# A recommendation tower on one NeuronCore: each VectorE product of 2,048 columns is written as four of 512

## The chip, the core and the metric

The kernel runs on one NeuronCore of a Trainium2 chip. TensorE multiplies matrices into PSUM, VectorE and ScalarE work element by element, GpSimd here only issues gathers from tables, and SyncE only issues DMAs. The five engines run their own instruction streams and meet through semaphores. The metric is the device time of one execution in microseconds (us); lower is better.

## What is computed

For each of 2,048 samples, 39 table rows of 32 floats are looked up. Two interaction layers form all products of the 39 fields per embedding column `d`, weight and sum them; their sums over `d` go through a three-layer perceptron. Everything is float32.

```python
e = stack([tbl_f[ids[:, f]] for f in range(39)], axis=1)          # (2048, 39, 32)
conv1 = einsum('bid,bjd,ijk->bkd', e, e, W1)                       # 39*39 pairs -> 128
hidden1, final1 = conv1[:, :64], conv1[:, 64:]
conv2 = einsum('bid,bjd,ijk->bkd', e, hidden1, W2)                 # 39*64 pairs -> 128
z = sum(concatenate([final1, conv2], axis=1), axis=2)              # (2048, 192)
h = relu(concatenate([z, dense_ctx], axis=1) @ W_top1 + b_top1)
y = relu(h @ W_top2 + b_top2) @ W_top3
```

## The kernel before

The samples are cut into 16 tiles of 128, and two tiles are a pair. A pair is worked on in four chunks (`k` = 0 to 3) of half a tile each, so there are 32 chunks. The first and the last pair are written out, and the pairs between run in hardware loops on each engine.

For `hidden1`, a chunk's values lie transposed in `x_rows[k % 2]`: 117 partitions (three copies of the 39 fields) by 2,048 columns (64 samples by 32). Three more arrays, `x_moved`, hold the same values with the fields rotated; they lie in a ring of four buffers (`CRING`). A chunk has seven steps. In steps 0 to 5 VectorE multiplies two of these four arrays (`PRODUCTS`, L658) and writes all products into one of four `blocks` buffers (`ZRING`); step 6 (L640) finishes a smaller array `last`. After each step the semaphore `multiplied` rises by one, and TensorE (`hidden_step`, L370) waits for it before its matmuls of that step; each of those four reads 512 of the 2,048 columns. VectorE runs three steps ahead of TensorE (`AHEAD`).

Between the steps VectorE also transposes the finished `hidden` of the chunk before (`turn_hidden`, L668, behind step 3), transposes a tile's embeddings (`turn_x`, L632) and copies small results. TensorE's second layer (`gram_group`, L390) waits for `hid_turned`, the signal of L668; ScalarE copies its results into `arena` (L556), from which TensorE forms the final sums (`final_sums`, L407).

All larger DMAs are issued in one fixed order by SyncE's queue, SPq. For every chunk it loads `x_rows` from a scratch array `turning` in HBM (L270), copies it within SBUF to the second and third copy (L277), waits until they have landed (L280), and issues nine DMAs of 312 KB for the three rotated `x_moved` (L290) and one for `last` (L299). For every tile it also spills the gathered embeddings to `turning` in two parts (L263) and waits for each. Its waits on computed data are these: in L286 for `multiplied` before an `x_moved` buffer is written again (for the second of the three: step 2 of the chunk before must be done; for the third: step 4), in `spill_and_turn` for `multiplied` and `last_squared` before `x_rows` is written again, and at L299 for `hid_steps`, the signal of TensorE's last step.

GpSimd issues 39 gathers per tile (L337); it starts a tile when its ids are there, VectorE has transposed the tile that lay in the buffer (`xt_ready`) and its spill has landed.

Of the kernel before, what the change touches and what calls it, by code (L numbers as in the profile page):

```python
# [33 lines left out]
ALU = mybir.AluOpType  # L34
# [4 lines left out]
D = 32  # L39
Q = 4  # L40
# [8 lines left out]
HALF = PLACES // 2  # L49
COLS = HALF * Q * D  # L50
THIRDS = 3
ROWS = THIRDS * F
# [19 lines left out]
ZRING = 4  # L72
# [15 lines left out]
def build(nc, dense, ids, tables, W_top1, b_top1, W_top2, b_top2, W_top3, W1, W2,  # L88
          fold_c, identf_c, turning, y_out):
    with ExitStack() as ctx:  # L90
        def sb(name, shape, dt):
            return ctx.enter_context(nc.sbuf_tensor(name, shape, dt))

        def sem(name):
            return ctx.enter_context(nc.semaphore(name))
# [7 lines left out]
        blocks = sb("blocks", [P, ZRING, COLS], F32)  # L103
# [71 lines left out]
        multiplied = sem("multiplied")  # L175
# [28 lines left out]
        def triples(k, p):  # L204

            if k % 2:
                return turns(k, p)
            return turns(k, p) + 2 * 16 * (1 if k == 0 and isinstance(p, int) and p == 0 else 2)
# [417 lines left out]
        def _(dve):  # L626
# [8 lines left out]
            def multiply(k, t, chunk, p):  # L635

                if t == STEPS - 1:
                    dve.wait_ge(last_moved, 16 * (chunk + 1))
                    rows = slice(LAST_AT, LAST_AT + F)
                    nc.vector.tensor_tensor(last[rows, :], x_rows[k % 2][rows, :], last[rows, :],  # L640
                                            ALU.mult).then_inc(multiplied, 1)
                    return
                if t < 3:

                    n = 3 * k + t
                    dve.wait_ge(moved[n % CRING], 16 * THIRDS * (3 * p + n // CRING + 1))
                if t == 0:
                    dve.wait_ge(tripled[k % 2], triples(k, p))
                if not (isinstance(chunk, int) and 6 * chunk + t < ZRING):

                    back = STEPS * chunk + t - ZRING + 1 if t >= ZRING else STEPS * (chunk - 1) + t + 6 - ZRING + 1
                    dve.wait_ge(hid_steps, back)

                def copy(u):
                    return x_moved[(3 * k + u - 1) % CRING][0:ROWS, :] if u else x_rows[k % 2][:, :]

                u, v = PRODUCTS[t]
                nc.vector.tensor_tensor(blocks[0:ROWS, (6 * k + t) % ZRING, :], copy(u), copy(v),  # L658
                                        ALU.mult).then_inc(multiplied, 1)

            def turn_hidden(k, chunk):

# [22 lines left out]
            def pair_body(p, first, last_pair):  # L685
                for k in range(4):
                    chunk = 4 * p + k
                    for t in range(STEPS):
                        kk, tt = (k, t + AHEAD) if t + AHEAD < STEPS else (k + 1, t + AHEAD - STEPS)
                        if not (last_pair and kk == 4):  # L690
                            multiply(kk, tt, 4 * p + kk, p)
                        if t == 0 and (k or not first):
                            turn_hidden((k - 1) % 4, chunk - 1)
                        if t == 3 and k % 2 == 0:
                            turn_x(2 * p + k // 2, k // 2, p + 1)
                        if t == 1 and k % 2 == 0 and not first:
                            final_copy(2 * p - 2 + k // 2)
                        if t == 3 and k % 2 and not first:
                            y_copy(2 * p - 2 + k // 2)
# [23 lines left out]
            for t in range(TILES):  # L723
                op = nc.vector.tensor_copy(
                    dense_rows[FIN1:FIN1 + DENSE, t * P:(t + 1) * P].rearrange("p (h r q) -> p q r h", h=2, q=Q),
                    hidden[0:DENSE, t // 8, t // 4 % 2, (t % 4) * P:(t % 4 + 1) * P].rearrange("p (q r h) -> p q r h", q=Q, h=2))
# [9 lines left out]
            for t in range(AHEAD):  # L736
                multiply(0, t, 0, 0)
# [55 lines left out]
```

## Time and profile before

| | us |
|---|---|
| median of 3 runs | 1284.77 |
| lowest and highest run | 1278.77, 1286.57 |
| span of the profiled execution | 1282.7 |
| TensorE matmul busy in it | 897.3 |
| GpSimd busy | 828.4 |
| ScalarE busy | 626.2 |
| VectorE busy | 621.8 |

The busy times are sums over the whole span; none of the four fills it. The page of the profile also follows the chain of work that ended last back from the end, step by step to what released each instruction, and gives shares of the span by engine and line.

### The profile page before, as it was taken

The page shows a single profiled execution, that of the slowest core. Times are in us where ns is not written, and L with a number is a line of the kernel's source. Part 1 is how long each engine was busy: PE and PEld are TensorE (multiplying, and loading weights), DVE is VectorE, ACT ScalarE, POOL GpSimd, SP SyncE. Part 2 cuts the span into 40 slices and gives each one's busy share as a digit, 9 for nine tenths or more (in the row PEclk, how much of TensorE's full clock was granted, in tenths as well). Part 3 has the DMA queues.
Part 4 walks back from the last instruction along what each step waited for, and adds up shares of the span by engine and source line. Part 5 has one row for each costly group of instructions (what it writes and reads, how often), then busy time and mean ns, then how long its engine had stood idle before and what let it go on. Part 6 is the DMA issues. An engine that isn't in the chain of part 4 may idle for free.

```text
span 1282.7 us, 14200 instructions
## 1 busy us (share of the span) xinstructions
PE 897.3 (70%) x4685; PEld 477.9 (37%) x4685; DVE 621.8 (48%) x401; ACT 626.2 (49%) x1553; POOL 828.4 (65%) x628
## 2 busy tenths in 40 slices
PE   3055578786767778786677787676777877687786
PEld 3011224342333435342433434343353534343366
DVE  3245254646536364555535464654536455463440
ACT  0003555553546564454646545355655444464653
POOL 7785888668884888658883888848884688810000
PEclk9557678887888888786878979688888878788888
DMA  7466756555565655555665555556555565665500
GB/s 199 63 140 139 138 136 132 128 130 126 135 140 130 133 131 128 124 133 127 144 127 128 129 131 131 128 131 138 128 133 126 126 133 122 135 143 119 120 1 1
DMA packets 145611, 159.96 MB, mean 125 GB/s; under 512 B 115027, under 2 KB 127779, under 8 KB 130643
## 3 DMA queue, kind: packets, MB, share of 16 engines
q1 hardware_dynamic: 125623, 149.45, 51.7%
q0 software_dynamic: 19968, 10.26, 4.7%
q8 instruction: 11, 0.18, 0.1%
q14 instruction: 9, 0.07, 0.0%
HBM read 28.00 MB, written 10.23 MB: 30 GB/s over the span
## 4 chain that ended last, share of the span: by engine, by line
SPq 46%; DMA 40%; issue 4%; PE 4%; POOL 3%; ACT 3%; DVE 1%; ACTq 0%; DVEq 0%
SPq L290 40%; DMA x_rows<-x_rows 15%; DMA x_rows<-turning 14%; DMA turning<-emb 10%; POOL emb L337 3%; SPq L270 3%; SPq L277 2%; ACT arena L556 2%; DMA x_moved<-x_rows 1%; PE gram L390 1%; PE fin L407 1%; SPq L303 1%; PE hidden L370 1%; DVE blocks L658 0%; ACT xdiag L539 0%
## 5 line engine op out<-in xcount | busy, mean ns | idle before, releaser
L337 POOL DMA_INDIRECT emb<-in_tbl,ids_tile x624 | 828.2, 1327 | 300.6 <-issue 196.4
L370 PE MATMUL hidden<-blocks,w_pairs 117*64 117x512 f32 x1536 | 495.2, 781 | 331.5 <-DVE blocks L658 331.3
L556 ACT ACTIVATE arena<-gram 32x240 f32<-32x240 f32 (+5 forms) x960 | 302.0, 315 | 529.5 <-PE gram L390 518.7
L658 DVE TENSOR_TENSOR blocks<-x_rows,x_moved 117x2048 f32<-117x2048 f32 x96 | 219.6, 2287 | 326.2 <-DMA x_moved<-x_rows 325.8
L370 PEld LDWEIGHTS hidden<-blocks,w_pairs 117*64 117x64 f32 x1536 | 123.7, 166 | 614.6 <-issue 306.6
L658 DVE TENSOR_TENSOR blocks<-x_moved 117x2048 f32<-117x2048 f32 x96 | 220.2, 2294 | 246.7 <-DMA x_moved<-x_rows 242.8
L390 PEld LDWEIGHTS gram<-xdiag,gst 128*103 128x103 f32 x1024 | 150.1, 185 | 114.1 <-issue 94.8
L390 PE MATMUL gram<-xdiag,gst 128*103 128x156 f32 x1024 | 175.3, 324 | 17.4 <-DVE gst L668 11.0
L539 ACT ACTIVATE xdiag<-gst 32x468 f32<-32x468 f32 (+1 forms) x256 | 119.2, 466 | 39.2 <-DVE gst L632 35.4
L407 PE MATMUL fin<-arena,w_fin 128*128 128x128 f32 x640 | 80.5, 284 | 2.6 <-ACT arena L556 2.6
L640 DVE TENSOR_TENSOR last<-x_rows,last 39x2048 f32<-39x2048 f32 x32 | 73.3, 2291 | 17.0 <-DMA last<-x_rows 16.4
L407 PEld LDWEIGHTS fin<-arena,w_fin 128*128 128x128 f32 x640 | 78.7, 201 | 2.7 <-ACT arena L556 2.7
L513 ACT ACTIVATE hid_high<-hidden 32x512 f32<-32x512 f32 x128 | 75.3, 588 | 7.1 <-PE hidden L370 5.3
L370 PE MATMUL hidden<-last,w_pairs 103*64 103x512 f32 x256 | 65.2, 607 | 6.8 <-DVE last L640 6.8
L527 ACT ACTIVATE last<-x_rows 39x2048 f32<-39x2048 f32 x32 | 61.0, 1905 | 0.4
L370 PEld LDWEIGHTS hidden<-last,w_pairs 103*64 103x64 f32 x256 | 26.2, 139 | 36.7 <-issue 19.0
L632 DVE STREAM_TRANSPOSE gst<-emb 128x1248 f32<-128x1248 f32 x16 | 39.6, 2476 | 0.5
L456 PE MATMUL fin<-act,wt 128*128 128x128 f32 x256 | 32.7, 281 | 8.8 <-ACT act L579 8.8
L519 ACT ACTIVATE hidden<-hidden 32x512 f32<-32x512 f32 x64 | 36.2, 566 | 1.4
L456 PEld LDWEIGHTS fin<-act,wt 128*128 128x128 f32 x256 | 29.8, 191 | 12.6 <-ACT act L579 12.6
L412 PE MATMUL fin<-arena,w_fin 128*64 128x128 f32 x384 | 30.9, 279 | 0.0
L527 ACT ACT_TABLE_LOAD x1 | 1.3, 1283 | 60.2 <-DMA x_rows<-turning 60.2
(44 smaller groups left out, 271.5 us busy)
## 6 DMA issues: line engine op xcount, KB each, us to landing
x_moved<-x_rows SPq DMA_DIRECT2D x288, 312.0 KB
x_rows<-x_rows SPq DMA_DIRECT2D x60, 312.0 KB
emb<-in_tbl,ids_tile POOLq DMA_INDIRECT x624, 4.5
last<-x_rows SPq DMA_DIRECT2D x32, 312.0 KB
x_rows<-turning SPq DMA_DIRECT2D x36, 208.0 KB
turning<-emb SPq DMA_DIRECT2D x16, 416.0 KB, 5.9
x_rows<-turning SPq DMA_DIRECT2D x36, 104.0 KB
turning<-emb SPq DMA_DIRECT2D x16, 208.0 KB, 3.2
```

The lines of the kernel that those rows point to most:

```text
L290: sp.dma_start(x_moved[slot][g * F:(g + 1) * F, :], x_rows[k % 2][r:r + F, :]).then_inc(moved[slot], 16)
L337: pool.indirect_dma_start(out=emb[u][:, f * D:(f + 1) * D], out_offset=None, in_=tables[f], in_offset=bass.IndirectOffsetOnAxis(ap=ids_til ...
L370: mm = nc.tensor.matmul(hidden[64 * c:64 * c + 64, k % 2, bank, :], w_pairs[0:rows, t, bank * HALF_HID:bank * HALF_HID + HID], block[:, 2 ...
L390: mm = nc.tensor.matmul(gram[0:GS, bank, r * GM:(r + 1) * GM], gst[k // 2][:, 2 * place + k % 2, 0:GS], xdiag[:, place, :], start=True, st ...
L407: mm = nc.tensor.matmul(fin_conv2, w_fin2[:, n, :], gram2[:, n, cols], start=(n == 0), stop=(n == FH - 1))
L456: mm = nc.tensor.matmul(outs2[:, m, :], wt2[:, c, m * P:(m + 1) * P], act1[:, c, :], start=(c == 0), stop=(c == T1 // P - 1))
L513: op = nc.scalar.activation(hid_high[32 * q:32 * q + 32, :], hidden[32 * other:32 * other + 32, k % 2, bank, :], ACT.Copy)
L527: nc.scalar.activation(last[0:F, :], x_rows[k % 2][0:F, :], ACT.Square).then_inc(last_squared, 1)
L539: op = nc.scalar.activation(xdiag[rows, places, q * F:(q + 1) * F], gst[k // 2][rows, 2 * places.start + k % 2:2 * places.stop:2, HID:GS], ...
L556: op = nc.scalar.activation(out[:, :, col:col + 2 * n].rearrange("p h (u b) -> p h u b", u=2), g[rows, i], ACT.Copy)
L640: nc.vector.tensor_tensor(last[rows, :], x_rows[k % 2][rows, :], last[rows, :], ALU.mult).then_inc(multiplied, 1)
L658: nc.vector.tensor_tensor(blocks[0:ROWS, (6 * k + t) % ZRING, :], copy(u), copy(v), ALU.mult).then_inc(multiplied, 1)
```

## The change

In `multiply`, the one `tensor_tensor` of a step 0 to 5 becomes four, each over a quarter of the columns. `Q` is 4, `HALF * D` is 512. The step's waits stand ahead of the first of the four, the one signal `multiplied` stands on the last. Step 6 stays one instruction of 2,048 columns.

```diff
                 u, v = PRODUCTS[t]
-                nc.vector.tensor_tensor(blocks[0:ROWS, (6 * k + t) % ZRING, :], copy(u), copy(v),
-                                        ALU.mult).then_inc(multiplied, 1)
+                for q in range(Q):
+                    cols = slice(q * HALF * D, (q + 1) * HALF * D)
+                    op = nc.vector.tensor_tensor(blocks[0:ROWS, (6 * k + t) % ZRING, cols], copy(u)[:, cols],
+                                                 copy(v)[:, cols], ALU.mult)
+                op.then_inc(multiplied, 1)
```

The instruction streams of the other engines are unchanged. On VectorE, the last chunk of the program before the change reads as follows; in brackets stand the semaphores that a row waits for:

```order
L658 TENSOR_TENSOR blocks<-x_moved 117x2048 [waits hid_steps,moved3]
L658 TENSOR_TENSOR blocks<-x_rows,x_moved 117x2048 [waits hid_steps]
L668 STREAM_TRANSPOSE gst<-hid_high 128x16x32 [waits gram_filled,hid_sorted]
L668 STREAM_TRANSPOSE gst<-hidden 128x16x32 [waits hid_sorted]
L658 TENSOR_TENSOR blocks<-x_moved 117x2048 [waits hid_steps]
```

It begins with step 2, behind the last `x_moved` to land. The same place after the change:

```order
L660 TENSOR_TENSOR blocks<-x_moved 117x512 [waits hid_steps,moved3]
L660 TENSOR_TENSOR blocks<-x_moved 117x512 x3
L660 TENSOR_TENSOR blocks<-x_rows,x_moved 117x512 [waits hid_steps]
L660 TENSOR_TENSOR blocks<-x_rows,x_moved 117x512 x3
L671 STREAM_TRANSPOSE gst<-hid_high 128x16x32 [waits gram_filled,hid_sorted]
L671 STREAM_TRANSPOSE gst<-hidden 128x16x32 [waits hid_sorted]
L660 TENSOR_TENSOR blocks<-x_moved 117x512 [waits hid_steps]
```

Nothing has changed places: each product stands as four rows where it stood as one, and the two transposes follow eight pieces instead of two products.

## Rows read from the trace of the kernel before

**Rows 1.** The page: busy time of the engines, and the chain that ended last.

```profile
PE 897.3 (70%) x4685; PEld 477.9 (37%) x4685; DVE 621.8 (48%) x401; ACT 626.2 (49%) x1553; POOL 828.4 (65%) x628
...
SPq 46%; DMA 40%; issue 4%; PE 4%; POOL 3%; ACT 3%; DVE 1%; ACTq 0%; DVEq 0%
SPq L290 40%; DMA x_rows<-x_rows 15%; DMA x_rows<-turning 14%; DMA turning<-emb 10%; POOL emb L337 3%; SPq L270 3%; SPq L277 2%; ACT arena L556 2%; DMA x_moved<-x_rows 1%; PE gram L390 1%; PE fin L407 1%; SPq L303 1%; PE hidden L370 1%; DVE blocks L658 0%; ACT xdiag L539 0%
```

**Rows 2.** Waits of SyncE's queue, whole run: total us, times, longest us.

```profile
SPq L280 <- DMA x_rows<-x_rows: 174.0, 30, 6.2
SPq L329 <- DVE y_row L748: 69.4, 1, 69.4
...
SPq L262 <- DMA emb<-in_tbl,ids_tile: 22.5, 2, 12.1
```

**Rows 3.** Timeline of SyncE's queue, pieces of 386 to 1211: start us, length us, what.

```profile
387.19 3.25 SPq L290 DMA_DIRECT2D x_moved<-x_rows  x3
...
572.45 17.48 SPq L290 DMA_DIRECT2D x_moved<-x_rows  x9
590.16 5.78 SPq L270 DMA_DIRECT2D x_rows<-turning  x2
596.05 0.80 SPq L299 DMA_DIRECT2D last<-x_rows  x1
...
1193.09 17.32 SPq L290 DMA_DIRECT2D x_moved<-x_rows  x9
```

**Rows 4.** Timeline of VectorE, pieces of 376 to 1061; in brackets its idle time.

```profile
376.95 2.29 DVE L658 TENSOR_TENSOR blocks<-x_moved 117x2048 f32<-117x2048 f32 x1 [1.69 <-DMA x_moved<-x_rows]
...
567.51 2.29 DVE L640 TENSOR_TENSOR last<-x_rows,last 39x2048 f32<-39x2048 f32 x1 [1.05 <-DMA last<-x_rows]
...
583.02 2.29 DVE L658 TENSOR_TENSOR blocks<-x_rows,x_moved 117x2048 f32<-117x2048 f32 x1 [13.03 <-DMA x_moved<-x_rows]
590.20 2.31 DVE L658 TENSOR_TENSOR blocks<-x_moved 117x2048 f32<-117x2048 f32 x1 [4.89 <-DMA x_moved<-x_rows]
596.24 2.29 DVE L658 TENSOR_TENSOR blocks<-x_moved 117x2048 f32<-117x2048 f32 x1 [3.73 <-DMA x_moved<-x_rows]
598.45 2.28 DVE L658 TENSOR_TENSOR blocks<-x_rows,x_moved 117x2048 f32<-117x2048 f32 x1
...
1058.43 2.29 DVE L658 TENSOR_TENSOR blocks<-x_rows,x_moved 117x2048 f32<-117x2048 f32 x1 [4.91 <-DMA x_moved<-x_rows]
```

**Rows 5.** TensorE's last step of a chunk, in its timeline at 576.

```profile
576.19 2.09 PE L370 MATMUL hidden<-last,w_pairs 103*64 103x512 f32 x8
```

**Rows 6.** Groups by line, VectorE: busy us, mean ns of one, idle before, releasers.

```profile
L658 DVE TENSOR_TENSOR blocks<-x_moved 117x2048 f32<-117x2048 f32 x96 | 220.2, 2294 | 246.7 <-DMA x_moved<-x_rows 242.8 <-PE hidden L370 3.8
L658 DVE TENSOR_TENSOR blocks<-x_rows,x_moved 117x2048 f32<-117x2048 f32 x96 | 219.6, 2287 | 326.2 <-DMA x_moved<-x_rows 325.8
...
L710 DVE TENSOR_TENSOR arena<-arena 128x768 f32<-128x768 f32 x1 | 1.0, 958 | 0.0
```

**Rows 7.** The chain of waits at the last chunk, 1208 to 1226.

```profile
1217.49 2.30 DVE blocks L658
...
1219.84 3.68 PE hidden L370 x8
1223.52 2.48 PE gram L390 x12
```

**Rows 8.** Timeline of VectorE at the same place.

```profile
1219.70 2.29 DVE L658 TENSOR_TENSOR blocks<-x_rows,x_moved 117x2048 f32<-117x2048 f32 x1
...
1222.53 0.68 DVE L668 STREAM_TRANSPOSE gst<-hidden 128x512 f32<-128x512 f32 x1
```

**Rows 9.** GpSimd: duration of its 624 gathers, and its timeline at 596.

```profile
L337 POOL DMA_INDIRECT emb<-in_tbl,ids_tile x624: 940/946/3046, 2.9 to 1128.3; - x156
...
597.38 1.97 POOL L337 DMA_INDIRECT emb<-in_tbl,ids_tile  x1 [0.30 <-issue]
599.65 1.89 POOL L337 DMA_INDIRECT emb<-in_tbl,ids_tile  x1 [0.30 <-issue]
```

## Prediction, written before the changed kernel was run

> **What bounds the kernel now.** I read the page first. No engine is busy for more than 70% of the span, so busy time does not say what sets it. The chain that ended last does: 46% of it is SyncE's queue and 40% DMAs in flight; VectorE has 1%, and L658, the line that changes, rounds to 0% [rows 1]. So the span is a single file of DMA work: issue nine `x_moved` copies, issue and await the next `x_rows`, copy it, await that, issue the next nine.
>
> The question is then whether this file ever waits for VectorE. The waits of SyncE's queue say no: in the whole run the engine behind its waits is VectorE only at L329, the store of the result at the very end; the others shown are all transfers [rows 2]. A wait that has been met before it is reached leaves no row, so I looked at how early it is met, in the two timelines side by side. There are four kinds.
>
> - The second `x_moved` of a chunk needs step 2 of the chunk before. I take the start of the first copy of the nine, which is earlier and so on the safe side. The tightest of the 31 places is the product of 376.95, over at 379.24, against 387.19: 7.95 us [rows 3, 4].
> - The third `x_moved` needs step 4, which starts two products and two transposes later, but its own copies are issued later too, behind six others.
> - `x_rows` at 590.16 needs the last product of the chunk before, over at 567.51 + 2.29 = 569.80: 20.4 us [rows 3, 4].
> - `last` at 596.05 needs TensorE's last step, over at 578.28: 17.8 us [rows 3, 5].
>
> VectorE itself waits for transfers: 13.03, 4.89 and 3.73 us before the first three products of the chunk at 583 [rows 4]. In the grouped rows this is 242.8 + 325.8 = 568.6 us, and behind TensorE it stood only 3.8 us [rows 6].
>
> **The change, part by part.** It adds 3 x 192 = 576 VectorE instructions and no column of work.
>
> *Price of one product.* A product of 2,048 columns lasts 2,287 to 2,294 ns; the same operation on 768 columns lasts 958 [rows 6]. The slope is (2,291 - 958) / 1,280 = 1.041 ns per column, which leaves 958 - 800 = 158 ns that do not depend on the length. One of 512 columns should last 0.69 us. Back to back it is less, since the record of an instruction overlaps the start of the next: 596.24 to 598.45 is a step of 2.21 us for an instruction of 2.29 [rows 4], an overlap of 0.08. So a piece takes 0.69 - 0.08 = 0.61 us, and four of them end after 3 x 0.61 + 0.69 = 2.52 us instead of 2.29: **+0.23 us per product**. The bounds are 0 (if the fixed part hid wholly) and 3 x 0.158 = +0.47 us (if nothing overlapped). I take 0.23, because both of its numbers are rows of this very operation.
>
> The Trainium skill speaks against this change: in "VectorE: DVE Perf Modes", section "The TRN2 errata", it says that SBUF latency is exposed between instructions and that many small tiles each pay it. Its section "The DRAIN you can't avoid" goes further: the next operation does not start until the pipeline has emptied. The trace does not quite bear out the latter, as the step is 0.08 us shorter than the recorded duration; by that rule the product would cost +0.47 us, by the rows +0.23.
>
> *What lies beside other work.* Over the run the price is 192 x 0.23 = 44 us of VectorE time. Almost all of it falls into idle time. Steps 0, 1 and 2 each wait for a transfer; a delay of 0.23 us in step 0 is gone at the next wait. From step 2 to step 5 four products run one behind the other, so what follows is 4 x 0.23 = 0.9 us late (`last`, `turn_x`). Then VectorE is idle before the next chunk's first product; the smallest of these idle times within the run is 4.91 us [rows 4]. Nothing is carried into the next chunk. For SyncE's queue the second `x_moved` needs a step that ends 0.23 us later and has 7.95 us to spare; the third needs step 4, 0.7 us later; `x_rows` needs `last`, 0.9 us later with 20.4 to spare. If that cover were gone, the whole 44 us would show. TensorE gets its blocks 0.23 to 0.9 us later, and its last step has 17.8 us to spare.
>
> *On the path.* One product is on the chain, step 2 of the last chunk at 1217.49 [rows 7]. TensorE's matmuls at 1219.84 wait for it: +0.23 us. Behind it is a second, nearly tied wait. The gram matmuls at 1223.52 need both the end of those matmuls and the transpose over at 1222.53 + 0.68 = 1223.21 [rows 7, 8]. The transpose stands behind two products and comes 0.46 us later, at 1223.67, while TensorE would be there at 1223.75. With the propagation of a signal it may win by a tenth. So the end moves by 0.23 to 0.5 us; I take 0.3. The steps behind it are queued on TensorE behind gram matmuls and final sums and have their blocks in time.
>
> *GpSimd.* A gather lasts 0.94 us at best, and its median is 0.946 [rows 9]. But the one begun at 597.38 lasted 1.97 and the one at 599.65 lasted 1.89. They ended at 599.35 and 601.54, each about 0.9 us behind the start of a new VectorE instruction (598.45, and the transpose behind the product's end at 600.73): a gather that meets a two-input product waits until that instruction is over, then needs its 0.9 us [rows 4, 9]. VectorE does not lose by it: the step to 598.45 is 2.21 us with a gather waiting. 624 gathers at 0.946 would be 590 us; the page has 828 [rows 1], so 238 us are this wait. With pieces of 0.61 us a gather waits at most 0.6 instead of 2.2. In an unbroken run of products one gather then goes through in 3 pieces (1.8 us) instead of one product (2.2), so it would last about 1.5 us instead of 1.9. This should bring GpSimd from 828 to about 720 us (650 to 760).
>
> The skill's page "SBUF — State Buffer", section "Who interferes with whom", states that a VectorE instruction with two SBUF inputs contends with a GpSimd one that reads SBUF, and that the loser blocks until the other is over; the durations above agree.
>
> It buys nothing at the end of the kernel: SyncE's queue waited for gathers twice, 22.5 us in all [rows 2], and both are the first tile's, before any product runs.
>
> **The sum.** 1282.7 + 0.3 = 1283.0 us on the time of the profiled execution, which lies 2.1 us below the median of the runs. Against the median it is 1284.77 + 0.3 = 1285.1. I forecast **1285 us**, no change.
>
> **The rivals.**
>
> *Slower: the added time lands on the path.* For this SyncE must be made to wait on `multiplied` in every chunk. The price is 192 x 0.23 = 44 us, time 1329 us (with +0.47 per product, 90 us and 1375). It decides once step 2 ends 8 us later than now, against 0.23 forecast; that would need each piece to lose microseconds, for instance to GpSimd taking its turn in every gap. Against it: the gaps it already uses cost VectorE nothing, and TensorE's and SyncE's margins are 8 to 20 us. Chance 5%.
>
> *Faster: gathers that finish sooner leave the DMA engines to the file.* A chunk with gathers and one without differ little: the nine `x_moved` issues take 17.48 us at 572.45 [rows 3], amid gathers, and 17.32 at 1193.09 [rows 3], behind the last gather, which began at 1128.3 [rows 9]. Each gather still moves the same bytes, only sooner. If the earlier end took 0.4 us off each of 32 chunks, it would be 13 us, 1272 us; more likely is 1 to 3 us. Chance of over 1%: 3%, of the small gain 7%.
>
> *The change does not do what it says.* The instruction rows show the four pieces with one signal, so this is out. If the fixed price were hidden, the time would be 1284.8, the same verdict.
>
> *No change:* the remaining 85%, with its own range of 1278 to 1291, as the three runs spread over 7.8 us and I add the bounds 0 and +0.5.
>
> **Chances.** About 1% (12.8 us) is what a measurement of this kernel can tell from no change. Faster by more 0.03, within 1% 0.92, slower by more 0.05. The range of 1277 to 1292 leaves out the slower rival, the large gain and the outermost runs.
>
> **What would show it.** In the profile of the changed kernel: L660 has 768 instructions of about 0.69 us; a product from its first start to its last end 2.52 us; VectorE busy about 90 us more where the pieces' durations are summed (768 x 0.69 - 440). The chain still has SyncE's queue and DMAs at 86% and no wait of SyncE on `multiplied`. VectorE's idle behind transfers shrinks by some 40 us. Gathers last at most about 1.6 us beside products; only beside step 6, still one instruction of 2,048 columns, some last up to 3. GpSimd is busy near 720 us. The prediction is wrong if the steps of SyncE's file get longer although it waits for no engine, if back-to-back pieces are spaced over 0.7 us, or if a row of SyncE's waits names L660 within the run.

## The result and the profile after

| | before | after |
|---|---|---|
| median of the runs, us | 1282.45 (18 runs) | 1290.86 (18 runs) |
| span of the profiled execution, us | 1282.7 | 1289.2 |

The ratio after to before is 1.0063, with a 95% interval of 1.0038 to 1.0087. By the bound of 1% this is no change, as forecast, and 1290.9 us lies in the range. But the interval leaves out 1.000: the kernel is about 8 us slower, where the sum said 0.3 us. One of the 18 runs before took 1512.76 us; the ratio leaves it out, and no trace of it was kept.

The page of the profile after shows the same bound. The first line is the busy time, the others the chain that ended last:

```profile
PE 891.2 (69%) x4685; PEld 477.2 (37%) x4685; DVE 663.2 (51%) x977; ACT 626.7 (49%) x1553; POOL 642.8 (50%) x628
...
SPq 46%; DMA 40%; issue 4%; POOL 3%; PE 3%; DVE 2%; ACT 2%; DVEq 0%; ACTq 0%
SPq L290 41%; DMA x_rows<-x_rows 14%; DMA x_rows<-turning 13%; DMA turning<-emb 11%; POOL emb L337 3%; SPq L270 3%; DMA x_moved<-x_rows 2%; SPq L277 2%; DVE blocks L660 1%; ACT arena L556 1%; PE gram L390 1%; PE fin L407 1%; SPq L303 1%; PE hidden L370 1%; DVE last L640 0%
```

SyncE's queue and its transfers are 86% of the chain, as in [rows 1]. GpSimd has gone from 828.4 to 642.8 us. The waits of SyncE's queue (total, times, longest) name no VectorE product and no TensorE step, as in [rows 2]:

```profile
SPq L280 <- DMA x_rows<-x_rows: 175.4, 30, 6.3
SPq L329 <- DVE y_row L751: 66.7, 1, 66.7
SPq L277 <- DMA x_rows<-turning: 65.7, 30, 4.1
...
SPq L262 <- DMA emb<-in_tbl,ids_tile: 21.7, 2, 12.5
```

The groups by line of VectorE (busy, mean ns, idle before) answer to [rows 6], and the timeline of the last chunk to [rows 8]:

```profile
L660 DVE TENSOR_TENSOR blocks<-x_rows,x_moved 117x512 f32<-117x512 f32 x384 | 243.6, 694 | 313.6 <-DMA x_moved<-x_rows 313.2
L660 DVE TENSOR_TENSOR blocks<-x_moved 117x512 f32<-117x512 f32 x384 | 240.1, 686 | 233.0 <-DMA x_moved<-x_rows 229.3 <-PE hidden L370 3.8
```

```profile
1224.58 2.50 DVE L660 TENSOR_TENSOR blocks<-x_moved 117x512 f32<-117x512 f32 x4 [3.02 <-DMA x_moved<-x_rows]
1226.99 2.49 DVE L660 TENSOR_TENSOR blocks<-x_rows,x_moved 117x512 f32<-117x512 f32 x4
1229.40 0.70 DVE L671 STREAM_TRANSPOSE gst<-hid_high 128x512 f32<-128x512 f32 x1
1230.03 0.68 DVE L671 STREAM_TRANSPOSE gst<-hidden 128x512 f32<-128x512 f32 x1
```

The chain of waits there answers to [rows 7]:

```profile
1227.13 3.68 PE hidden L370 x8
1230.81 0.12 issue
1230.93 1.90 PE gram L390 x12
```

From the start of step 2 to the gram matmuls it is 1230.93 - 1224.58 = 6.35 us, and was 1223.52 - 1217.49 = 6.03. From step 2 to the end of the span it is 64.6 us, and was 65.2. So the end of the kernel did what was said and holds none of the loss. The profiled execution's 6.5 us came earlier, in SyncE's file. The first nine `x_moved` copies of the kernel and those of chunk 31 start here (before the change 62.62 and, in [rows 3], 1193.09):

```profile
64.30 17.24 SPq L290 DMA_DIRECT2D x_moved<-x_rows  x9
...
1201.68 17.19 SPq L290 DMA_DIRECT2D x_moved<-x_rows  x9
```

That is 1137.4 us for 31 cycles against 1130.5, 6.9 us more, and 1.7 us more ahead of it; behind it the profiled execution is 2.1 us shorter. The question is why a file that waits for no engine became longer.

### The profile page after: what moved, and what is told of

Read it like the earlier page. It is cut to its first block, busy times and chain, and to the rows that moved or that the text cites. A ratio compares the mean times of both kernels' runs of the same rounds, so it can differ in the third digit from the quotient of the medians.

```text
span 1289.2 us, 14776 instructions
## 1 busy us (share of the span) xinstructions
PE 891.2 (69%) x4685; PEld 477.2 (37%) x4685; DVE 663.2 (51%) x977; ACT 626.7 (49%) x1553; POOL 642.8 (50%) x628
## 4 chain that ended last, share of the span: by engine, by line
SPq 46%; DMA 40%; issue 4%; POOL 3%; PE 3%; DVE 2%; ACT 2%; DVEq 0%; ACTq 0%
SPq L290 41%; DMA x_rows<-x_rows 14%; DMA x_rows<-turning 13%; DMA turning<-emb 11%; POOL emb L337 3%; SPq L270 3%; DMA x_moved<-x_rows 2%; SPq L277 2%; DVE blocks L660 1%; ACT arena L556 1%; PE gram L390 1%; PE fin L407 1%; SPq L303 1%; PE hidden L370 1%; DVE last L640 0%
## 5 line engine op out<-in xcount | busy, mean ns | idle before, releaser
L337 POOL DMA_INDIRECT emb<-in_tbl,ids_tile x624 | 642.6, 1030 | 470.6 <-DMA ids_tile<-in_ids 244.4
L370 PE MATMUL hidden<-blocks,w_pairs 117*64 117x512 f32 x1536 | 486.6, 768 | 335.0 <-DVE blocks L660 335.0
L660 DVE TENSOR_TENSOR blocks<-x_rows,x_moved 117x512 f32<-117x512 f32 x384 | 243.6, 694 | 313.6 <-DMA x_moved<-x_rows 313.2
L660 DVE TENSOR_TENSOR blocks<-x_moved 117x512 f32<-117x512 f32 x384 | 240.1, 686 | 233.0 <-DMA x_moved<-x_rows 229.3
L390 PE MATMUL gram<-xdiag,gst 128*103 128x156 f32 x1024 | 175.4, 324 | 25.1 <-DVE gst L671 17.8
L539 ACT ACTIVATE xdiag<-gst 32x468 f32<-32x468 f32 (+1 forms) x256 | 119.2, 466 | 41.2 <-DVE gst L632 37.4
L370 PEld LDWEIGHTS hidden<-last,w_pairs 103*64 103x64 f32 x256 | 26.1, 139 | 36.5 <-issue 19.0
```

The costliest lines, as they stand in the source:

```text
L337: pool.indirect_dma_start(out=emb[u][:, f * D:(f + 1) * D], out_offset=None, in_=tables[f], in_offset=bass.IndirectOffsetOnAxis(ap=ids_til ...
L370: mm = nc.tensor.matmul(hidden[64 * c:64 * c + 64, k % 2, bank, :], w_pairs[0:rows, t, bank * HALF_HID:bank * HALF_HID + HID], block[:, 2 ...
L390: mm = nc.tensor.matmul(gram[0:GS, bank, r * GM:(r + 1) * GM], gst[k // 2][:, 2 * place + k % 2, 0:GS], xdiag[:, place, :], start=True, st ...
L539: op = nc.scalar.activation(xdiag[rows, places, q * F:(q + 1) * F], gst[k // 2][rows, 2 * places.start + k % 2:2 * places.stop:2, HID:GS], ...
L660: op = nc.vector.tensor_tensor(blocks[0:ROWS, (6 * k + t) % ZRING, cols], copy(u)[:, cols], copy(v)[:, cols], ALU.mult)
```

## The experiments

Two theories stood against each other. Theory G: the gathers, no longer held back, come closer together and slow SyncE's transfers. Theory V: the pieces cost the time themselves. Four sets of kernels ran, each set on one chip with runs of the kernel before beside it. That kernel took 1340, 1351, 1344 and 1284 us there. The first three chips behave in a way that the first comparison did not show; this became a finding of its own. Each chip was used for one set at one time, so whether the chip or the hour makes the difference is not shown. No trace of the kernel before was kept on these chips.

| set | kernel | median, us | ratio to before | interval |
|---|---|---|---|---|
| 1 | a third of the gathers, whole products | 1316.1 | 0.9832 | 0.9789 to 0.9874 |
| 1 | a third of the gathers, four pieces | 1326.3 | 0.9902 | 0.9868 to 0.9937 |
| 1 | four pieces, three clears ahead of a gather | 1422.3 | 1.0656 | 1.0589 to 1.0723 |
| 1 | whole products, three clears behind each | 1344.0 | 1.0033 | 0.9997 to 1.0069 |
| 2 | four pieces | 1562.5 | 1.1609 | 1.1540 to 1.1678 |
| 2 | sixteen pieces | 1580.0 | 1.1730 | 1.1637 to 1.1823 |
| 2 | a third of the gathers, sixteen pieces | 1324.9 | 0.9850 | 0.9797 to 0.9903 |
| 2 | whole products, three clears behind each | 1367.8 | 1.0151 | 1.0067 to 1.0235 |
| 3 | four pieces | 1551.0 | 1.1550 | 1.1501 to 1.1599 |
| 3 | four pieces, increments ahead of a gather | 1294.7 | 0.9668 | 0.9620 to 0.9716 |
| 4 | whole products, increments ahead of a gather | 1285.1 | 1.0015 | 0.9982 to 1.0048 |
| 4 | four pieces, increments ahead of a gather | 1294.5 | 1.0078 | 1.0051 to 1.0105 |

**A third of the gathers (set 1).** From the second pair on only every third field is gathered, and the waits for gathers count accordingly. The other fields keep old values, so this kernel computes something else and serves for timing alone.

```diff
-                    look_up(u)
+                    look_up(u, range(0, F, 3))
```

With whole products:

> Products whole, as before the change. From the second pair on only 13 of a tile's 39 gathers are issued (this leaves the other fields of those tiles stale, and with them the results). Theory G (the change costs 8 us because unblocked gathers come closer together and hold up SyncE's transfers): gathers have a price for SyncE's file, so taking two thirds of them away makes it faster, by 10 to 25 us, about 1262 us. Theory V (the 8 us are VectorE's added time, somewhere on the path) says nothing on this kernel alone.

With four pieces:

> The same third of the gathers, products in four pieces; its output lacks the same fields. Theory G: against the kernel with whole products and a third of the gathers the pieces cost a third of 8 us or less, 0 to 3 us. Theory V: they cost the whole 8 us again.

Two thirds of the gathers less took 24 us off (1340.5 to 1316.1), but on this chip that is not their price to the file alone, since with all gathers TensorE is disturbed as told below. From chunk 2 to chunk 31 the file takes 1040.4 us here, and with all gathers 1058.3 and 1049.7 in the two undisturbed traces of whole products (before, and set 4): 9 to 18 us, across chips. The pieces cost 10.2 us here, although only 13 gathers per tile were left; theory G allowed 3. The start of the nine copies of chunk 2 and of chunk 31 are 184.91 and 1225.27 with whole products, and with four pieces 184.65 and 1234.40. So 29 cycles take 1040.4 and 1049.8 us: the 9 us are again in the file. The two intervals of the ratios overlap a little, since each holds the noise of the kernel before; the runs themselves do not (whole products 1313.0 to 1319.7, pieces 1320.9 to 1328.2). This speaks against theory G.

**Whole products with a later signal (sets 1 and 2).** Behind each product VectorE clears three small areas, and the last carries the signal. It was meant to come as late as with pieces.

```diff
-                                        ALU.mult).then_inc(multiplied, 1)
+                                        ALU.mult)
+                for i in range(3):
+                    op = nc.vector.memset(extra[:, (6 * k + t) % ZRING, i, :], 0.0)
+                op.then_inc(multiplied, 1)
```

> Products whole, and behind each VectorE clears three columns groups of 24 in a spare tile, so that a product's signal comes about 0.25 us later, as with four pieces, while a gather still waits up to 2.2 us. Theory G: no change, ratio 0.998 to 1.003. Theory V: 1.006, about 1290 us.

> Whole products with three small clears behind each, again, since in the first set TensorE was slow on that chip. Theory G: ratio 0.998 to 1.003. Theory V: 1.005 to 1.008.

The results are 1.0033 and 1.0151. The three clears are shorter than expected:

```profile
603.31 2.29 DVE L659 TENSOR_TENSOR blocks<-x_rows,x_moved 117x2048 f32<-117x2048 f32 x1 [5.35 <-DMA x_moved<-x_rows]
605.55 0.14 DVE L662 MEMSET extra<- 128x24 f32 x3
```

Over the 192 products the signal comes 2.37 us behind a product's start, 0.08 us later than in the kernel before (2.29) and not the 0.25 us that was aimed at. Both chips also had the disturbance told of next. So these two runs do not say what VectorE's lateness costs, neither the 8 us nor the 16%.

**The changed kernel again (sets 2 and 3).** The same program as in the first comparison. The second expectation has one reading wrong: TensorE's gaps in set 2 are mostly some 2 us long and not 0.7, and they sum to 473 us where it has 421.

> The changed kernel once more, beside the others of this set. Ratio to before 1.004 to 1.009, as measured first (1.0063).

> The changed kernel a third time. So far 1.006 on the first chips and 1.161 on one where TensorE issued its instructions about 0.7 us apart towards the end of each tile's gathers. Either the one or the other is expected, with such gaps in the trace if it is the latter (0 us of issue idle on TensorE in the first trace, 421 us in the second).

It took 1562.5 and 1551.0 us, 16% over the kernel before on the same chips. This is what the prediction had no room for. Two groups of TensorE by line, first after the change in the first comparison, then in set 2 (busy, mean ns, idle before, what ended it):

```profile
L412 PE MATMUL fin<-arena,w_fin 128*64 128x128 f32 x384 | 30.9, 279 | 0.0
...
L473 PE MATMUL misc<-arena 128*128 128x64 bf16 x252 | 9.6, 208 | 15.8 <-DMA arena<-in_fold 15.2 <-issue 0.6
```

```profile
L412 PE MATMUL fin<-arena,w_fin 128*64 128x128 f32 x384 | 56.3, 305 | 144.2 <-issue 144.1
...
L473 PE MATMUL misc<-arena 128*128 128x64 bf16 x252 | 18.5, 220 | 101.4 <-issue 86.1 <-DMA arena<-in_fold 15.3
```

"Issue" is time in which TensorE waited for nothing that the profile shows. The timeline shows how it looks (start, length, what, and idle before):

```profile
375.21 0.37 PE L412 MATMUL fin<-arena,w_fin 128*64 128x128 f32 x1 [2.63 <-issue]
378.33 0.37 PE L412 MATMUL fin<-arena,w_fin 128*64 128x128 f32 x1 [2.75 <-issue]
381.20 0.37 PE L412 MATMUL fin<-arena,w_fin 128*64 128x128 f32 x1 [2.50 <-issue]
```

One matmul in 2.8 us, of a group that otherwise runs back to back. The stretches of one such place, with the gathers of a tile lasting from 345.4 to 397.1 (columns: stretch, length, busy time and count of each engine, granted clock, DMA share, GB/s):

```profile
345.00:370.00 25.00, 22.44 (x124) 14.58 (x124) 12.93 (x20) 9.05 (x24) 19.26 (x18) 0.84 0.55 119
370.00:402.00 32.00, 5.28 (x15) 2.49 (x15) 9.99 (x16) 1.01 (x2) 20.84 (x21) 0.55 0.35 75
402.00:418.00 16.00, 15.72 (x71) 9.31 (x72) 11.89 (x15) 12.41 (x32) 0.00 (x0) 0.82 0.50 114
```

For the first 25 us of the gathers TensorE is at full pace, then it issues 15 matmuls in 32 us, and it recovers 5 us after the last gather. Over the kernel such gaps longer than 0.4 us sum to 473 us, and 461 of them begin between a tile's first gather and 5 us behind its last. The granted clock is 0.55 in that stretch, in which TensorE is busy for 5.28 of 32 us, and 0.84 and 0.82 beside it. The clock does not make the gaps: the matmuls between them still last only 0.37 us. SyncE's file then does wait for TensorE (total, times, longest; L297 stands just behind the wait for `hid_steps` ahead of `last`, L287 behind that for `multiplied`):

```profile
SPq L297 <- remote: 112.1, 6, 20.0
SPq L297 <- PE hidden L370: 73.8, 8, 20.0
...
SPq L287 <- DVE blocks L660: 48.8, 5, 11.0
```

The margin of 17.8 us in the prediction is eaten by some 30 us of slow issue, and SyncE waits up to 20 us at a time. The three rows are 234.7 us. The first `last` waits 51.4 us more (L299), because TensorE folds the weights late. Together that is the size of the loss: the span is 275.3 us longer than in the first comparison.

**Sixteen pieces (set 2).**

```diff
-                for q in range(Q):
-                    cols = slice(q * HALF * D, (q + 1) * HALF * D)
+                for q in range(16):
+                    cols = slice(q * COLS // 16, (q + 1) * COLS // 16)
```

> Each product in sixteen pieces of 128 columns, by the rows of before 0.21 us each, so a product ends about 1.2 us later than whole (four pieces: 0.23). Theory G (8 us by gathers that come closer together): gathers are hardly faster than with four pieces (1.03 us now, 0.95 at best), so the ratio stays at 1.005 to 1.010. Theory V (the cost follows VectorE's added time or instructions): five times 8 us, ratio about 1.03. Slack alone: 1.000 plus 1 to 2 us at the end of the kernel, since 4 x 1.2 us still fits into the smallest idle time of 4.91 us.

> Sixteen pieces, and from the second pair on only a third of the gathers (the other fields of those tiles stay stale). With a third of the gathers four pieces cost 10 us over whole products on a chip on which TensorE was slow. Theory V: about 40 us over whole products with a third of the gathers, ratio to before above 1.01. Theory G: the pieces cost at most 3 us here, ratio to before 0.98 to 0.99.

With all gathers sixteen pieces took 1580 us, a little over the four (1562.5) on the same chip, so 15 added instructions per product are not five times as bad as 3. With a third of the gathers the same sixteen pieces took 1324.9 us, 0.985 of the kernel before: the whole 16% needs both pieces and gathers. The page of that kernel gives VectorE 818.6 us busy:

```profile
PE 898.2 (68%) x4685; PEld 499.4 (38%) x4685; DVE 818.6 (62%) x3281; ACT 626.3 (47%) x1553; POOL 299.1 (23%) x264
```

That is 160 us more than with four pieces and a third of the gathers (658.3), and the time is the same (1324.9 and 1326.3), though on two different chips. Its file, from chunk 2 (184.66) to chunk 31 (1231.65), takes 1047.0 us, against 1049.8 with four pieces and 1040.4 with whole products. So the idle time of VectorE did hide its added work, and theory V in the form "in proportion to VectorE's time" falls: it asked for about 40 us over whole products, and the file shows 7. Sixteen pieces did not run on a chip without the disturbance.

**Gathers further apart (sets 1, 3 and 4).** First three small clears on GpSimd ahead of each gather:

```diff
                 for f in range(F):
+                    for i in range(3):
+                        op = pool.memset(pace[:, u, f, i:i + 1], 0.0)
+                    if f == F - 1:
+                        op.then_inc(paced, 1)
                     pool.indirect_dma_start(
```

> Products in four pieces, and GpSimd clears three single columns of a spare tile ahead of each gather, so that gathers come about 0.3 us further apart, as they did with whole products (mean 1.33 us). Theory G: the 8 us are gone, ratio to before 0.998 to 1.003. Theory V: the ratio stays at 1.006, 1290 us.

The clears hardly spaced the gathers. They fitted into the 0.3 us between two, and a tile's gathers took 54 to 58 us, where the changed kernel took 48 to 52 in sets 2 and 3. The ratio is 1.066; with the disturbance of set 1 it tells nothing of the 8 us. It does lie between the 1.16 of denser gathers and the 0.97 below of sparser ones, on another chip each. Then semaphore increments that nothing waits for:

```diff
                 for f in range(F):
+                    for i in range(10):
+                        pool.sem_inc(paced[i % 2], 1)
                     pool.indirect_dma_start(
```

> The changed kernel, with ten semaphore increments of no meaning ahead of each gather on GpSimd, so that gathers are as far apart as with whole products (a tile in 60 to 70 us; 51 us with pieces alone; three small clears did not do it, they fitted into the gap that is there). Theory G': the density of the gathers costs the time. On a chip without the issue gaps the 8 us go away (ratio 0.998 to 1.003); on a chip with them the 1.16 falls to 1.03 or less. Theory V: the four pieces themselves cost it, and the ratio stays where that of the changed kernel is.

On the chip of set 3, where the changed kernel takes 1551.0 us, this takes 1294.7, 0.967 of the kernel before. A tile's gathers take about 64 us there, since pauses appeared between them, some 100 of them longer than 1 us; the timeline of GpSimd:

```profile
640.35 1.22 POOL L340 DMA_INDIRECT emb<-in_tbl,ids_tile  x1 [0.32 <-issue]
643.34 0.95 POOL L340 DMA_INDIRECT emb<-in_tbl,ids_tile  x1 [1.78 <-issue]
```

TensorE's gaps are gone from the final sums and mostly from the folding of the weights (busy, mean ns, idle, releasers):

```profile
L415 PE MATMUL fin<-arena,w_fin 128*64 128x128 f32 x384 | 30.8, 279 | 0.2 <-issue 0.2
...
L476 PE MATMUL misc<-arena 128*128 128x64 bf16 x252 | 17.6, 239 | 28.9 <-issue 14.7 <-DMA arena<-in_fold 14.2
```

144.1 us of idle (126.6 in set 3, on this same chip) have become 0.2, and 86.1 (85.6) have become 14.7. The trace still puts 169.3 us down to issue at the hidden products, one stretch of them 36.5 us long. But the idle time ahead of the matmuls on `blocks` is 311.3 us in all here and 335.0 in the first comparison, where all of it is a wait for VectorE; so most of the 169.3 are probably waits whose releaser the trace did not catch. With sixteen pieces and a third of the gathers the group of the final sums (L416 there) has no idle either. So on these chips TensorE's gaps hang on the density and number of gathers, and the pieces act through them: they take away the wait that had spaced the gathers. The pauses on GpSimd are of the size of TensorE's gaps, so its own instructions may be slowed in the same way; what the two share was not found.

**The same with whole products (set 4).** Ten increments in the first two tiles, three later.

> The kernel before, with semaphore increments ahead of the gathers: ten in the first two tiles, where no product holds gathers back, and three later, where whole products do. Theory G': where TensorE shows issue gaps in the kernel before (1344 us), they go away here too, first of all the 85 us while it folds the weights, and the time falls to 1280 to 1300 us. If four pieces have a small cost of their own (the 8 us of the first comparison), this kernel is 5 to 10 us faster than the paced one with pieces; if that too came from the gathers, the two are within 3 us.

> The changed kernel with ten semaphore increments ahead of each gather, again, on the same chip as whole products with spaced gathers: 1290 to 1300 us, ratio 0.96 to 0.97 where the kernel before takes 1344 us, and 1.00 where it takes 1282.

This chip had no issue gaps, and the kernel before took 1284.1 us. The increments also did nothing here: gathers start 1.25 us apart, as without them, in the kernel with pieces:

```profile
60.75 0.94 POOL L340 DMA_INDIRECT emb<-in_tbl,ids_tile  x1 [0.30 <-issue]
62.00 0.94 POOL L340 DMA_INDIRECT emb<-in_tbl,ids_tile  x1 [0.31 <-issue]
```

So the expectation that they would space the gathers failed, and this pair cannot test theory G. The increments do lengthen GpSimd's program: instruction queue q14 moves 78 packets here and 79 in set 3, and 11 in the changed kernel. As both runs have them, they alone do not make the pauses of set 3. What it gives is a second measurement of the change on an undisturbed chip: 1.0078 with pieces against 1.0015 with whole products, 9.4 us between the medians. SyncE's waits for the spill, whole products first (total, times, longest):

```profile
SPq L269 <- DMA turning<-emb: 49.4, 20, 4.4
SPq L267 <- DMA turning<-emb: 46.7, 12, 6.7
```

```profile
SPq L269 <- DMA turning<-emb: 53.9, 20, 5.3
SPq L267 <- DMA turning<-emb: 51.7, 12, 5.9
```

They are 96.1 and 105.6 us. In the first comparison the same sum was 101.2 and 102.8. Adding the durations of SyncE's instructions, from the same timelines, makes the two pairs agree. This is what the 31 cycles hold (a cycle goes from one chunk's first `x_moved` copy to the next one's):

| sum over 31 cycles, us | before | whole, increments | after | four pieces, increments |
|---|---|---|---|---|
| all | 1130.5 | 1124.3 | 1137.4 | 1143.3 |
| spills: issue and wait | 132.0 | 129.1 | 138.7 | 139.0 |
| issue of the nine `x_moved` copies | 514.9 | 512.2 | 518.4 | 517.7 |
| issue of the loads of `x_rows` | 98.1 | 96.3 | 99.6 | 100.2 |
| loads of the ids | 13.9 | 15.6 | 9.9 | 11.6 |

Between the means of the two kinds the cycles grow by 13.0 us: 8.3 at the spills, 4.5 and 2.7 at the two other issues, and the ids give 4.0 back. So no one wait is longer, but nearly every step that issues or awaits a large DMA is, the spills most. The rest of the span, outside the 31 cycles, is 152 to 154 us in all four.

To tell the two theories apart all the same, I took the same 31 cycles in each of the four undisturbed traces, and looked at the 15 that hold a spill:

| mean of a cycle with a spill, us | before | whole, increments | after | four pieces, increments |
|---|---|---|---|---|
| the 7 with at most 14 gathers ended in them | 38.20 | 38.06 | 38.65 | 38.70 |
| the 8 with more | 39.19 | 39.09 | 39.74 | 39.78 |

More gathers go with a cycle longer by 1 us in all four, and the pieces add 0.5 to 0.7 us in both rows. The 16 cycles without a spill are 34.35 and 34.08 us with whole products, 34.31 and 34.64 with pieces: no growth in one pair, 0.6 us in the other. A fit over all 124 cycles, with a slope for the number of gathers and a step for a spill, gives the pieces 0.42 us per cycle with a standard error of 0.12 (0.23 and 0.62 in the two pairs). By 31 that is 13 us, as these four traces differ; the medians differ by 8 to 9.

That the cycles with few gathers grew too speaks against closer gathers as the cause. It is not a clean test, since those few stand closer together as well. Set 1 is cleaner: with a third of the gathers, at most 13 in a cycle, the 29 cycles from chunk 2 on are 0.32 us longer with pieces, with a standard error of 0.11, little less than with all gathers.

## Why the prediction came out as it did

- *What bounds the kernel.* Right, and seen again: no wait of SyncE's on `multiplied` or `hid_steps` within the run where TensorE is undisturbed. Two readings were loose. The waits for VectorE are not at L329 alone: one of 0.4 us stands at the start, for `w_fin` (L222). And 20.4 and 17.8 us are the margins of one chunk each; over the trace of before the smallest are 13.1 for `x_rows` and 10.7 for `last`.
- *Price of one product.* Right. The pieces last 0.686 and 0.694 us (0.69 forecast), and a product 2.52 us on average over all 192 (2.52 forecast), +0.23 us. By the rule of the Trainium skill ("VectorE: DVE Perf Modes", section "The DRAIN you can't avoid") that the pipeline empties before the next operation starts it would have been 2.77; this trace does not agree with it. Without a gather beside it a product is 2.49 us, beside gathers 2.53 on average and at most 2.61, so GpSimd costs VectorE 0.04 us per product and at most some 0.1.
- *What lies beside other work.* Right for VectorE: its idle behind `x_moved` shrank from 568.6 to 542.5 us, 26 where some 40 were forecast, and its idle ahead of `last` from 17.0 to 8.7. With a third of the gathers sixteen pieces, with 160 us more of VectorE time, cost no more than four.
- *On the path.* Right: +0.32 us from step 2 to the gram matmuls, 0.23 to 0.5 forecast.
- *GpSimd.* The direction was right and the size wrong: 643 us, where 720 (650 to 760) was forecast. The step that failed is that a gather beside pieces waits for three of them and lasts 1.5 us. Most do not wait at all: 64 of 624 last over 1.2 us, where 193 did. The first of these two begins with a piece of the product of 601.40, which runs to 603.96, and does not wait; the second is one of the 64:

```profile
601.38 0.95 POOL L337 DMA_INDIRECT emb<-in_tbl,ids_tile  x1 [0.30 <-issue]
...
607.63 1.44 POOL L337 DMA_INDIRECT emb<-in_tbl,ids_tile  x1 [0.30 <-issue]
```

- *The sum.* It said +0.3 us, and +8.4 us was measured between the medians (ratio interval 0.4 to 0.9%). The terms for the engines held; the one that was missing is a lengthening of SyncE's own cycles. I had taken the transfers' time as given, once no wait named an engine. The prediction itself named this as a sign of being wrong: "if the steps of SyncE's file get longer although it waits for no engine". That is what happened. The forecast "no change" holds only because 8 us are less than 1%; for a term that the sum did not have, that is luck.
- *The rivals.* The slower one had the wrong mechanism on the undisturbed chips (nothing waits on `multiplied`). On the two other chips on which the changed kernel ran, the loss (207 us in set 3) is over four times its price of 44, and its last step, SyncE made to wait, is what happens. But the wait is mostly on TensorE, through gathers set free, which I had counted as a possible gain only.

What stays open is how pieces lengthen the file on an undisturbed chip. The undisturbed traces exclude a wait on an engine. The runs with a third of the gathers exclude proportion to VectorE's time or to the number of pieces, as far as two chips can be compared. They speak against the gathers' density (cycles with few gathers grew too, and with a third of the gathers the cost was still 10 us). The added time lies in issuing and awaiting large DMAs, the spills most. What the transfers meet was not found, and what a later signal alone does was not tested, since the run meant for it came only 0.08 us later.

A version that beats both everywhere was not found. On the chip of set 3 pieces with increments are the fastest that ran (0.967); on that of set 4 whole products are. Whole products with increments were run only where there was nothing to gain (1.0015). Whether they bring the kernel before from 1344 to 1285 on the other chips was not tried.

## What to carry to other kernels

When a change frees an engine off the critical path, ask what it will issue faster and who shares that; here the freed gathers cost 16% on two chips, against 0.3 us forecast for all the arithmetic of VectorE. Time a small change on more than one chip before it is called neutral: the same two programs stood at 1.006 and at 1.16. And a file of transfers that waits for no engine can still get longer when an engine beside it changes, so its cycles have to be measured and not only cleared of waits.

## What the hardware showed that was not expected

- On three of the chips TensorE paused between matmuls beside dense gathers, down to one matmul in about 2.8 us. In the changed kernel of set 2 four in five of the gaps longer than 0.4 us are 1.0 to 2.9 us long. It happens with whole products too: the folding of the weights, from 14.1 to 24.1 us in the kernel before in the first comparison, ran from 14.2 to 119.2 us in set 1 with whole products. In most tiles the rows of gaps start 15 to 27 us after the gathers begin and end 3 to 9 us behind the last; single gaps come earlier. The cause within the chip was not found; in set 2 the instruction queues moved nothing between 480 and 1470 us, while the gaps went on.
- A gather often waits for a two-input VectorE instruction of 2.2 us (mean of all gathers 1.33 us) and mostly not for one of 0.6 us (mean 1.03 us, 0.94 at best).
- Ten semaphore increments on GpSimd between two gathers cost nothing on one chip (a tile in 51 to 55 us) and spaced them to 58 to 65 us per tile on another.
